# A hybrid scan, attention and expert kernel: the order of the small matmuls in the attention stage

## What is computed

```python
def performer_causal_attention(q, k, v):          # q, k, v: [B, S, H=16, DH=16]
    phi_q = jax.nn.relu(q) + KERNEL_EPS
    phi_k = jax.nn.relu(k) + KERNEL_EPS
    kv = jnp.cumsum(jnp.einsum('bshm,bshd->bshmd', phi_k, v), axis=1)
    num = jnp.einsum('bshm,bshmd->bshd', phi_q, kv)
    den = jnp.einsum('bshm,bshm->bsh', phi_q, jnp.cumsum(phi_k, axis=1))
    return num / den[..., None]
```

## Time and profile before

| | |
|---|---|
| median of 3 runs | 2596.24 us (2581.92, 2596.24, 2597.45) |
| the profiled execution | 2582.66 us |
| its span | 2580.9 us |
| PE, PEld, DVE, ACT, POOL busy | 88%, 75%, 76%, 28%, 31% |
| mean granted clock of TensorE | 0.865 |

### The profile page before, as it was taken

One profiled execution on the slowest core, in us unless ns is written; L12 is line 12 of the kernel. 1 busy time (PEld: TensorE's weight loads), 2 busy tenths in 40 slices (PEclk: granted clock), 3 DMA queues, 4 the chain that ended last, 5 costly groups with the idle time before them and its releaser, 6 DMA issues. The chain is left out here.

```text
span 2580.9 us, 57102 instructions
## 1 busy us (share of the span) xinstructions
PE 2263.5 (88%) x16096; PEld 1935.7 (75%) x16096; DVE 1972.6 (76%) x6529; ACT 726.6 (28%) x1656; POOL 808.6 (31%) x1042
## 2 busy tenths in 40 slices
PE   7836787989899998989899998989899899989997
PEld 3413666878888887878778887878788778878887
DVE  3559848879797878878796878888887979788532
ACT  3430203222232313232332313232222323132423
POOL 0040203233332324233332424242333423142524
PEclk9865768889898988989897988989897989889988
DMA  7530100010000001000000101010000101010000
GB/s 266 184 105 15 27 5 20 10 26 11 15 24 11 23 10 28 11 23 11 25 14 11 27 7 27 11 26 12 23 11 11 27 8 27 10 27 6 5 1 9
DMA packets 101085, 74.21 MB, mean 29 GB/s; under 512 B 64376, under 2 KB 94592, under 8 KB 99712
## 3 DMA queue, kind: packets, MB, share of 16 engines
q1 hardware_dynamic: 100736, 70.08, 9.8%
HBM read 46.43 MB, written 23.59 MB: 27 GB/s over the span
## 5 line engine op out<-in xcount | busy, mean ns | idle before, releaser
L1389 DVE TENSOR_TENSOR decayed_state<-state,decay 128x128 f32<-128x128 f32 x2048 | 682.1, 374 | 35.4 <-issue 31.3
L787 POOL TENSOR_TENSOR hs_parts<-hs_whole,hs_parts 128x256 fp32r<-128x256 f32 x640 | 486.6, 772 | 547.6 <-ACT hs_whole L911 466.1
L1399 DVE CUSTOM_DVE_ANT_0 state<-decayed_state,bank 128x128 f32<-128x128 f32 x2048 | 506.0, 286 | 31.2 <-PE bank L1001 17.3
L911 ACT ACTIVATE hs_parts<-bank,f_b_sb 128x256 fp32r<-128x256 f32 x512 | 245.3, 479 | 756.7 <-PE bank L1083 756.6
L1001 PE MATMUL bank<-xrows,brows 128*128 128x256 f32 x1024 | 269.0, 355 | 147.4 <-DVE state L1399 83.0
L1083 PE MATMUL bank<-f_w_hi,hs_parts 128*128 128x256 f32 x2048 | 344.1, 291 | 10.4 <-DVE x L1486 9.9
L1001 PEld LDWEIGHTS bank<-xrows,brows 128*128 128x128 f32 x1024 | 185.7, 225 | 201.4 <-issue 112.3
L1083 PEld LDWEIGHTS bank<-f_w_hi,hs_parts 128*128 128x128 f32 x2048 | 279.3, 190 | 53.1 <-ACT hs_parts L911 47.6
L811 POOL TENSOR_TENSOR kv<-kv,kvm 128x272 f32<-128x272 f32 x64 | 48.8, 763 | 675.5 <-DVE kvm L1598 675.5
L911 ACT ACTIVATE hs_whole<-bank,f_b_sb 128x256 f32<-128x256 f32 x512 | 245.8, 480 | 0.0
L1083 PE MATMUL bank<-late_fT_parts,f_w_hi 128*128 128x256 f32 x1024 | 188.4, 318 | 0.5 <-DVE kvm L1598 0.5
(11 more groups left out here) (154 smaller groups left out, 3563.6 us busy)
## 6 DMA issues: line engine op xcount, KB each, us to landing
xrows<-xs_dram SPq DMA_DIRECT2D x512, 32.0 KB
brows<-bs_dram SPq DMA_DIRECT2D x1024, 2.0 KB
xt<-in_x SPq DMA_DIRECT2D x4, 1024.0 KB, 7.9
xn_dram<-xn SPq DMA_DIRECT2D x4, 1024.0 KB, 5.6
z_dram<-zT SPq DMA_DIRECT2D x4, 1024.0 KB, 4.1
f_w_sb<-in_f_w SPq DMA_DIRECT2D x2, 2048.0 KB
xs_dram<-xhi SPq DMA_DIRECT2D x4, 1024.0 KB, 4.5
xs_dram<-xlo SPq DMA_DIRECT2D x4, 1024.0 KB, 7.3
```

What stands on the lines that cost most here:

```text
L787: return pool.tensor_tensor(lo, whole, hi.bitcast(f32), ALU.subtract)
L911: act.activation(slot[:, m], HB[e % 2][:, m * TOK:(m + 1) * TOK], ACT.Relu, bias=g["f_b1"][:, e, m:m + 1]).then_inc(done.sem, 1)
L1389: dve.tensor_tensor(decayed_state[:, part], state[:, (s - 1) % RING, part], decay[:, part], ALU.mult).then_inc(decayed.sem, 1)
L1399: dve._custom_dve(add_sat, out=state[:, s % RING, part], in0=decayed_state[:, part], in1=U[n % 2][:, s % 2 * D + h * HALF:s % 2 * D + (h + ...
```

## The change

The scores are issued group by group, and within a group slot by slot, so that each matmul is in another 32 rows than the one before it; all 16 stand together, and the `scan` that stood among them (A) comes behind them. The wait for `k_copied` stood ahead of slot 3, the 13th of 16 matmuls; it is now ahead of the 4th. `v_copied` (first tile) and `kv_masked` (second tile) are waited for ahead of the first. L1299 alternates between the two halves of columns, and L1316 between the two halves of rows.

```diff
-                    for hh in range(GH):
-                        if hh == 3:
-                            pe.wait_ge(k_copied.sem, k_copied.after(c, tile + 1))
-                        elif tile and hh < 2:
-
-                            pe.wait_ge(kv_masked.sem, kv_masked.after(c, hh + 1))
-                        elif not tile and hh == 2:
-                            pe.wait_ge(v_copied.sem, v_copied.after(c, TILES))
-                        for gr in range(GROUPS):
+                    if tile:
+                        pe.wait_ge(kv_masked.sem, kv_masked.after(c, 2))
+                    else:
+                        pe.wait_ge(v_copied.sem, v_copied.after(c, TILES))
+                    for gr in range(GROUPS):
+                        for hh in range(GH):
+                            if gr == 0 and hh == 3:
+                                pe.wait_ge(k_copied.sem, k_copied.after(c, tile + 1))
                             last = pe.matmul(SB[hh][:, gr * P:(gr + 1) * P], kT[PADH * hh:PADH * (hh + 1), gr, tok],
                                              qT[PADH * hh:PADH * (hh + 1), gr, tok], start=True, stop=True)
-                        last.then_inc(scored.sem, 1)
-
-                        if hh == 1:
-                            scan(1)
+                            if gr == GROUPS - 1:
+                                last.then_inc(scored.sem, 1)
+                    scan(1)
...
                     W = GH * HV
-                    for bb in range(2):
-                        b = 2 * tile + bb
-                        for gr in range(GROUPS):
+                    for gr in range(GROUPS):
+                        for bb in range(2):
+                            b = 2 * tile + bb
                             pe.matmul(OB[0][CT * bb:CT * (bb + 1), gr * W:(gr + 1) * W],
...
-                    for b in (2 * tile, 2 * tile + 1):
-                        part = slice(CT * (b % 2), CT * (b % 2 + 1))
-                        for gr in range(GROUPS):
+                    for gr in range(GROUPS):
+                        for b in (2 * tile, 2 * tile + 1):
+                            part = slice(CT * (b % 2), CT * (b % 2 + 1))
                             last = pe.matmul(HB[b % 2][:, gr * W:(gr + 1) * W], ktok[part, tile, gr * P:(gr + 1) * P],
                                              vv[part, tile, gr * GH:(gr + 1) * GH, :], start=True, stop=True)
-                        last.then_inc(kv_made.sem, 1)
+                            if gr == GROUPS - 1:
+                                last.then_inc(kv_made.sem, 1)
```

## The result

The changed kernel takes 2623.17 us (median of 4 runs, 2611.26 to 2626.41) against 2590.76 us (4 runs) of the kernel before: a ratio of 1.0125, 95% interval 1.0082 to 1.0167. The profiled execution took 2626.28 us, 43.6 more than that of before.

What follows compares the result with a forecast made beforehand. DVE's chain up to C was taken to bound each tile, so packing gains nothing there; 14 chunks at +3.1 us (+43), less 5 for the first and 4 for the last, make +34, hence 2620 us, range 2567 to 2655.

Steps and rivals of the forecast that it cites:

- Four slots run side by side: Scores on PE: four slots in rotation take 0.9 us a tile instead of 2.9; rival of no packing 0.08.
- DVE's chain: Masks and scan pairs ahead of C, 5.89 us of DVE: nothing quicker on PE ahead of C makes C earlier.
- PE waits 1.20 us at B: PE's scan call B after the scores: reached at about 3.5 us, A' ends at 4.6, some 1.2 us of waiting.
- First mask: DVE's first mask starts 1.8 us behind the first score instead of 1.19, from the moved key-copy wait: +0.6 us.
- L1299: Products after A, two halves of columns side by side: 0.3 us shorter, bound 0 to 0.5.
- Key-value products: L1316 with two chains of 8: -0.9 to -1.0 us a tile, -1.0 at half clock.
- Early fall of the clock in the first tiles: PE's clock falls at or before C in nearly every first tile: +3.1 us; forecast's chance 0.42.
- A chunk: Each of 14 of the 16 chunks costs 3.1 us more, +43 in all.
- First chunk: Clock is low during its scores and PE, not DVE, is late: gains about 5 us.
- the second tile: Clock low from L1307's second half on already; C at half clock +0.8, with +0.6 and -1.0: +0.4 us.
- the clock stays as it is: Rival: the clock falls where it did; -0.2 us a tile, -15 us in all, 2567 to 2581 us; chance 0.25.
- The counts of 4 and 9: Score instructions in the 0.43 us before and behind slot 0's giving way to slot 1, read as two slots interleaving.

Runs made afterwards that it cites:

- slot3_last: Changed kernel, but slots 0 to 2 rotate and slot 3's four matmuls come last, behind the key-copy wait: 2563.71 us, 0.9981 of the kernel before.
- two_and_two: Changed kernel, but slots 0 and 1 rotate, then A, then slots 2 and 3, key-copy wait ahead of slot 3: 2580.75 us, 1.0034 of the kernel before.
- products_only: Kernel before with only L1299 and the key-value products alternating, scores and A as they were: 2571.89 us, 1.0024 of the kernel before.
- wait_only: Kernel before, matmul and scan order unchanged, with the change's waits moved ahead: 2607.39 us, 1.0108 of the kernel before.
- scores_only: Kernel before with only the scores rotated and A behind them, both kinds of products as before: 2624.63 us, 1.0231 of the kernel before.
- filled: Changed kernel plus useless dense matmuls ahead of B and C, where PE waits: 2538.22 us, 0.9910 of the kernel before.
- slot3_filled: Changed kernel with slot 3's matmuls last and useless dense matmuls ahead of B and C: 2524.03 us, 0.9814 of the kernel before.

## Why the prediction was right

**Its main steps held.** Four slots run side by side: four starts some 7 ns apart, and the next four 0.11 us behind them, 28 ns each instead of 0.11 us; with the end, where slot 3 runs alone, the mean behind the pause is 35 ns, 3.1 times denser. The Trainium skill gives 3.07 times for four row tiles of 32 rows and 512 columns ("TensorE: Matmul & The Clock Gate", "Measured speedup vs the span model"); the 3.1 here are close to it, for another shape (128 columns, a load for each), and between the pause and slot 3's tail the trace has 4. The gain is then lost at DVE's chain, as forecast: PE waits 1.20 us at B (1.2 were forecast) and 0.74 at C (1.1), in the first tile, and DVE's idle time ahead of the first mask is 3.08 us (3.1). `slot3_last` shows the same without the pause: packed scores move C by 0.1 us. What the Trainium skill says in "TensorEngine Tiling (Array Packing)", "PSUM Bottleneck", that after such a speedup the emptying of PSUM may become the limit, is what these rows show, with the scan pairs on DVE added to the masks.

**The terms.** First mask: +0.6 forecast, +0.41 and +0.55 measured in the first and second tile from the first score, which in the first tile waits for the values and starts later as well. L1299 0.29 us shorter (0.3). Key-value products 0.91 us shorter at half clock (1.0). Early fall of the clock in the first tiles: 14 of 14 (nearly every one), second tile's start 25.55 us behind the first's (25). A chunk: +3.4 us (3.1). First chunk: 155.7 instead of 160.9 us to the next one's first score, -5.2 (-5).

**Terms that were off, and luck.** For the second tile I wrote that the clock is low from L1307's second half on already, and charged 0.4 us. It fell in the first half of it, 3.4 us earlier than before, and C came at 7.9 to 8.0 us in 13 of 14. In the mean of 13 chunks the stretch from the second tile's first score to the next chunk grew by 1.4 us (119.8 to 121.2), not 0.4, and that from the first tile to the second by 2.0 us (23.5 to 25.6), not 2.7: it is 3.0 us longer than the 22.6 of an undisturbed tile, but three of those tiles had the early fall before the change. The two errors cancel: a chunk came out 0.3 us from the forecast. At the end, the last but one chunk grew by 6.8 us (121.6 to 128.4), where I had charged 3.1, and the last one lost 6.9 us (103.4 to 96.4), where I had 4. The 43.6 us of the profiled executions are so 44.4 for 13 chunks, 6.8, -5.2 for the first chunk, -6.9, and +4.6 ahead of the first score, where nothing was changed and which differs by up to 8 us among the kernels profiled here. My sum was 34. That 2620 us came within 3 us of the median is luck, and the range of 2567 to 2655 held "the clock stays as it is" as well; what bears the prediction out is the waits, the place of C and the falls, not the time.

**Two readings of rows were wrong.** The counts of 4 and 9 from the earlier trace rows hold instructions that had started before their window; those that start in the two stretches of 0.43 us are 3 and 7. Two slots still run side by side, so nothing hangs on it. And thirteen score matmuls stand behind the wait for `k_copied`, not twelve; slot 3 had four.

**What I expected wrongly afterwards.** I held the early fall to be the packing's and the pause to cost only its length. `slot3_last` (0.9981) and `two_and_two` (1.0034) speak against it: they have packed scores without the pause, and stand within 0.5% of `products_only` (1.0024), which has their products and the old scores. The pause without the packing costs 1.1% (`wait_only`), with it 2.3% (`scores_only`). So the pause is what made the packed scores expensive, and packed scores make the pause dearer.

**Shown, and not shown.** Shown: that the clock is the price in the main (0.9910 with dense filling of 1.1 us a tile, 1.0131 with light filling of 1.9 us in the same places); that packing can't bring C forward while DVE's order stays; that the products' gain shows only with filling (0.9840 against 0.9963). Not shown: what the packed scores do without the pause when the products are as before, since both kernels without the pause have the alternating ones; and why a shift of 0.1 us in `wait_only` costs 1%.

## What to carry to other kernels

Before making an engine quicker, look at what it will wait for next: here the time saved ended up as waiting, 1.20 and 0.74 us in the first tile, for a chain on DVE that had been 0.15 us from being the bound. Where TensorE's matmuls become fewer or denser in front of a wait, read the granted clock of the stretch behind it in several repetitions, not in one; where it falls early in some repetitions and not in others, as in 3 of 14 here, a change that saves time can cost more than it saves. A wait that is long true in one place of an in-order queue needn't be so nine matmuls earlier: move matmuls, but leave the one that needs the wait last.

## What the runs showed of the hardware

Useless dense matmuls in waiting time made a kernel 2.1% faster relative to the kernel before than the changed one it was made from (0.9910 against 1.0125), and the best one with filling is 1.9% faster than the kernel before; matmuls of 17 columns in the same places, though they took 1.9 us a tile instead of 1.1, left it at 1.0131. The mean granted clock went from 0.840 to 0.887 (`filled`) and 0.882 (`slot3_filled`). Four row groups ran side by side with a weight load for every matmul: 26 pairs of f32 load and matmul, each load with 128 columns, started every 35 ns in the mean and every 28 ns while all four ran, where pairs in one row group need 0.11 us. Between the last start of one array shape and the first of the next lay 0.2 us (scores, then the scan's inputs).
